# Wq's first half issued ahead of ScalarE's function table, transposed tile 1 loaded by GpSimd's queue

## The reference

```
xn = (x - mean(x)) / sqrt(var(x) + 1e-5)
# branch 1: retrieval from a memory; only every 4th of the 32 heads of q is used
q    = (xn @ Wq.T + bq)[heads 0, 4, 8, ... 28]      # 8 heads of 128
s    = elu(q) + 1
a    = (s @ M) / (s @ z + 1e-6)                     # per head
attn = repeat(a, 4 heads) @ Wo.T
# branch 2: dense layer with int8 weights
dense = xn @ (w * w_scale) + b
out   = x + attn + dense
```

## Time and profile before

| | |
|---|---|
| median of three runs | 237.84 us (237.77 to 237.99) |
| the profiled execution's own time | 237.95 us |
| its span, first to last instruction | 236.1 us |
| TensorE matmul busy | 232.5 us, 98% |
| VectorE busy | 174.0 us, 74% |
| ScalarE busy | 125.2 us, 53% |
| GpSimd busy | 107.4 us, 45% |

### The profile page before, as it was taken

The page is one execution under the profiler, slowest core; times in us unless marked ns, Lnnn a source line. Parts: engine busy times, 40 slices in busy tenths (PEclk is TensorE's granted clock), DMA queues, the critical chain, the costliest instruction groups (busy, mean ns, idle before and its releaser), DMA issues.

```text
span 236.1 us, 3421 instructions
## 1 busy us (share of the span) xinstructions
PE 232.5 (98%) x1037; PEld 188.4 (80%) x1037; DVE 174.0 (74%) x275; ACT 125.2 (53%) x285; POOL 107.4 (45%) x117
## 2 busy tenths in 40 slices
PE   8999999999999999999999999999999999999995
PEld 3688788888888788888888888888888888888895
DVE  2989999897589987997858859585667879362511
ACT  4845358687298386585547253654637445630300
POOL 1029437856932356558350442524045598480000
PEclk9999999999999999999999999999999999999999
DMA  6999999999590144471727272431134456879521
GB/s 227 389 412 414 356 250 254 224 212 218 133 278 17 41 95 130 96 180 48 175 89 178 72 196 77 91 104 39 52 94 97 136 135 159 191 189 182 193 98 44
DMA packets 24081, 38.76 MB, mean 164 GB/s; under 512 B 5440, under 2 KB 13248, under 8 KB 22912
## 3 DMA queue, kind: packets, MB, share of 16 engines
q1 hardware_dynamic: 18816, 26.10, 33.7%
q0 software_dynamic: 3808, 11.14, 24.5%
q10 hardware_dynamic: 1440, 1.31, 1.9%
HBM read 25.95 MB, written 4.19 MB: 128 GB/s over the span
## 4 chain that ended last, share of the span: by engine, by line
PE 98%; DVE 0%; issue 0%
PE attn_ps L876 14%; PE attn_ps L878 14%; PE attn_ps L877 13%; PE q_ps L876 10%; PE q_ps L878 10%; PE q_ps L877 10%; PE dense_ps L876 6%; PE dense_ps L878 6%; PE dense_ps L877 6%; PE dense_ps L967 2%; PE q_ps L916 1%; PE q_ps L904 1%; PE q_ps L911 1%; PE attn_ps L916 1%; PE attn_ps L904 1%; PE attn_ps L911 1%
## 5 line engine op out<-in xcount | busy, mean ns | idle before, releaser
L489 ACT ACTIVATE s<-s,rden 128x128 f32<-128x128 f32 x128 | 39.2, 390 | 39.3 <-DVE rden L707 37.6
L341 POOL TENSOR_TENSOR e_and_sz<-s,z_b 128x512 f32<-128x512 f32 x32 | 41.7, 1340 | 39.6 <-DVE den L703 39.6
L876 PE MATMUL attn_ps<-P_hi,aT_hi 128*128 128x512 f32 (+1 forms) x136 | 53.0, 389 | 0.0
L878 PE MATMUL attn_ps<-P_hi,aT_lo 128*128 128x512 f32 (+1 forms) x136 | 52.2, 384 | 0.0
L877 PE MATMUL attn_ps<-P_lo,aT_hi 128*128 128x512 f32 (+1 forms) x136 | 52.1, 383 | 0.0
L876 PE MATMUL q_ps<-WqT_hi,xT_hi 128*128 128x512 f32 x104 | 40.7, 391 | 0.0
L878 PE MATMUL q_ps<-WqT_hi,xT_lo 128*128 128x512 f32 x104 | 40.5, 389 | 0.0
L877 PE MATMUL q_ps<-WqT_lo,xT_hi 128*128 128x512 f32 x104 | 40.5, 389 | 0.0
L691 DVE SCALAR_TENSOR_TENSOR q_ps<-q_ps,rstd,bq_b 128x512 f32<-128x512 f32 x28 | 21.0, 752 | 17.6 <-PE q_ps L878 17.6
L876 PEld LDWEIGHTS attn_ps<-P_hi,aT_hi 128*128 128x128 f32 x136 | 25.6, 188 | 6.1 <-issue 0.6
L878 PEld LDWEIGHTS attn_ps<-P_hi,aT_lo 128*128 128x128 f32 x136 | 25.6, 188 | 5.2
(11 more groups left out here) (96 smaller groups left out, 356.1 us busy)
## 6 DMA issues: line engine op xcount, KB each, us to landing
x<-in_WoT POOLq DMA_DIRECT2D x6, 1024.0 KB, 11.0
x<-in_b POOLq DMA_DIRECT2D x16, 256.0 KB, 4.4
out<-x SPq DMA_DIRECT2D x15, 256.0 KB, 2.4
x<-in_x SPq DMA_DIRECT2D x14, 256.0 KB, 3.6
xT<-in_xT SPq DMA_DIRECT2D x13, 256.0 KB, 3.8
aT<-s SPq DMA_DIRECT2D x104, 32.0 KB, 2.3
MT<-s SPq DMA_DIRECT2D x72, 32.0 KB, 1.9
x<-in_WoT SPq DMA_DIRECT2D x2, 1024.0 KB, 13.3
```

The source lines that it names most:

```text
L341: nc.gpsimd.tensor_tensor(sz_eps[:, :, h * D // 2:(h + 1) * D // 2].rearrange("p g (j c) -> p j g c", j=2), by_quarter(sbuf_s[:, t % SRING ...
L489: last = nc.scalar.activation(a_g, a_g, ACT.Copy, scale=rden[:, t % 2, g:g + 1])
L876: nc.tensor.matmul(out, x_hi, w_hi, start=start, stop=False)
L878: return nc.tensor.matmul(out, x_lo, w_hi, start=False, stop=stop)
```

## The change

ScalarE issues the load of Wq's half (0, 0) as its very first instruction, ahead of the wait for `warm` and of the function table. Transposed tile 1 leaves ScalarE's queue and becomes the first instruction of GpSimd's list, ahead of the constants. In its place ScalarE issues Wq's half (1, 0), which SP issued third before. SP's queue has one transfer fewer, and all that stands behind it moves up by one place. No arithmetic is changed.

```diff
@@ SyncE
             load_xT(0)
             load_wq_half(0, 1)
-            load_wq_half(1, 0)
             load_wq_half(1, 1)
@@ GpSimd
+            nc.gpsimd.dma_start(xT[:, 1, :, :].rearrange("p k r -> p (k r)"), xT_d[1]).then_inc(xT_in[1], 16)
             nc.gpsimd.memset(mean_weights, 1.0 / HID).then_inc(mean_weights_set, 1)
@@ ScalarE
+            act.dma_start(WqT_raw[:, 0, halves(0)], WqT_d[0, 0][:, halves(0)]).then_inc(wq_half_in[0], 16)
             act.wait_ge(warm_set, 1)
             nc.scalar.activation(table_loaded[:], warm[:, 0:1], ACT.Copy)
-            act.dma_start(WqT_raw[:, 0, halves(0)], WqT_d[0, 0][:, halves(0)]).then_inc(wq_half_in[0], 16)
-            act.dma_start(xT[:, 1, :, :].rearrange("p k r -> p (k r)"), xT_d[1]).then_inc(xT_in[1], 16)
+            act.dma_start(WqT_raw[:, 1, halves(0)], WqT_d[0, 1][:, halves(0)]).then_inc(wq_half_in[2], 16)
             copy_wq_hi(0, 0)
```

## The result

The changed kernel takes 239.27 us (median of six, 239.11 to 239.48), beside 237.98 us before in the same comparison. The ratio is 1.0054, 95% interval 1.0044 to 1.0065: slower by 1.3 us, where I had forecast no change at 237.9 us and a range up to 238.7. The profiled execution took 239.31 us, its span 237.5 us (236.1 before).

The account below looks back on a forecast made before the run. The prediction took TensorE's matmul stream as the bound, its early holes being VectorE's work. Its terms, 0 + 0 + 0 + 0 = 0, left 237.95 us, or 237.84 against the median: forecast 237.9 us, range 237.6 to 238.7.

Parts of the forecast that it names:

- Can this transfer hurt tile 0: Start of the kernel: half (0, 0) issued together with tile 0 delays it by 0, range up to 0.7 to 1.3 us.
- the row of ScalarE's latency: Earlier trace: ScalarE's issue at 169.85 has first packets from 171.05, 1.2 us or more later; from 0.74, 1.94 or later.
- Rival A: VectorE's first addition: half (0, 0) gets in front of tile 0, price 0.7 to 1.3 us, 238.5 to 239.1; chance 0.20.
- The prediction's next paragraph: DMA engines at the start: queues with work take turns by packet; the worst case is the first rival's time.
- TensorE's stream decides: Whole kernel: only TensorE's stream start or holes move the end; about 0.77 us of holes before 10.04 are VectorE's work.
- Half (0, 0) sooner gains 0: ScalarE's start: landing 0.24 us sooner gains 0, since ScalarE would still wait for VectorE at 5.61.
- Tile 1 from GpSimd, value 0: GpSimd's first transfer: issued at 0.74, packets about 2.35; tile 1 has 0.65 us of cover, so value 0.
- Rival B: Tile 1 gets before half (0, 0), or GpSimd's first issue is far slower than 1.6 us: 0.2 to 0.6 us; chance 0.12.
- GpSimd's constants, the table load, half (1, 0): Start: constants have 2.5 us of cover, the table load is hidden before 4.75, half (1, 0) gains nothing; each 0.
- VectorE is full behind it: After the first addition: once tile 0 is more than about 0.05 us late, everything moves with it.

Follow-up runs that it names:

- the half first: Kernels issuing Wq's half (0, 0) ahead of ScalarE's wait and table load, with or without other edits; that edit alone against the kernel before: 239.26 us, again 238.37.
- this part alone: Kernel before with only Wq's half (0, 0) issued ahead of ScalarE's wait and table load: median 239.26 us, ratio 1.0037.
- the kernel with GpSimd held: Changed kernel with GpSimd's product for w waiting until VectorE has made tile 2's low part: median 239.05 us, ratio 1.0038; on another chip 238.91 us.
- the half change: The change without its first part, half (0, 0) issued behind wait and table load as in the kernel before: median 238.47 us, ratio 1.0016.

## Why the prediction was wrong

The step that failed is the one in "Can this transfer hurt tile 0": "I take 0 as the value nearest to the row of ScalarE's latency". The measured value is 1.1 us in the changed kernel's profile, inside the bounds of 0.7 to 1.3 us that the same step gave, and 0.6 to 1.3 us over all profiles with the half first. The experiment with this part alone shows it. Rival A named the place and the price; it had 0.20.

The latency itself was read rightly. The step said that q10's packets come at 1.94 us or later, and in the changed kernel they begin after 2.3 us, in the other profiles with the half first after 2.0. What was wrong is the conclusion, that a queue which comes second costs the first one nothing. By 2.7 us q1 had started only 59 packets (77 with this part alone) where it had started 108, and q10 took its turns while tile 0 was unfinished. I thought of sharing as a matter of who is first; beside q10 tile 0 is slow for as long as both run. The prediction's next paragraph sets out that the queues take turns, which fits these counts; there it stood only as a worst case.

A second term is missing: 239.27 us lies above even rival A's top of 239.1. The prediction put nothing for VectorE's meeting with GpSimd's product, some 0.4 us by the kernel with GpSimd held.

Point by point:

- TensorE's stream decides, and the holes up to 10 us are VectorE's: right. A start 0.82 us later closed the stream 0.81 later, and VectorE was busy for all of that stretch but 0.03 us.
- Half (0, 0) sooner gains 0: right. In the changed kernel's profile it did not even land sooner.
- Tile 1 from GpSimd, value 0: wrong in the half change, by 0.42 us of wait (0.4 us in time). The issue came at 1.27, not 0.74, and the first packet 3.5 us or more after it, not 1.6: the earlier trace rows is a later transfer of that queue. Rival B named just this, a first issue far slower than 1.6 us, and its 0.2 to 0.6 us held. That the value is 0 in the whole change is luck: VectorE, late for another reason, comes to tile 1 at 7.58, after its landing at 7.0.
- GpSimd's constants, the table load, half (1, 0): 0, right as far as the traces show; the matrix for the mean is there at 2.2 us.
- "VectorE is full behind it", so everything moves one for one: incomplete. Two things on the way are not tied to the start. The clock gave back 0.27 us in the profiled execution, and took some more in others. GpSimd's product hangs on a landing; the shifted VectorE fell behind it. The prediction looked for what is hidden beside VectorE's list, not for what may overtake it.
- The sum for rival A: its price of 0.7 to 1.3 us gives a middle of 238.8, not 238.6, so a range up to 238.7 took in a third of A and not its lower half.

The sum as measured in the profiled execution: 1.12 (landing) - 0.30 (clock and the eight zeros' end) + 0.6 (what the lag grows by later, some 0.4 of it the meeting) gives the span's 1.4; the medians differ by 1.29.

## What to carry to other kernels

The first transfer on which all else waits should have the DMA engines to itself: do not issue one of another queue at the same moment. But do not hold the others back far either: here 0.24 us of head start were enough for tile 0, and with 1.5 us the half of Wq landed 4.4 us later and the kernel took 241.41 us. A latency read in the middle of a program held for ScalarE's first transfer and not for GpSimd's. A second queue that comes later than the first still takes its share. When a step on a full engine shifts, look for the instructions of other engines that hang on something that does not shift, above all GpSimd's long ones beside VectorE: a shift of a few tenths of a microsecond that turned the order there went with 1 us. And when two kernels agree in their times, look whether the same thing set both.

## What the runs showed of the hardware

- Two hardware queues with work at the start share the engines: with the half of Wq issued beside tile 0, q1 and q10 started 77 and 36 packets from 1.7 to 2.7 us where q1 alone started 108. Together they could move as much as one: 412 GB/s from 4 to 5 us in the changed kernel. With ScalarE's transfers issued late it was 269 GB/s from 5 to 7 us; why is open.
- A transfer of 256 KB took 2.7, 3.8, 5.7 or 6.8 us to land, by its queue, its moment and what was beside it.
- GpSimd's first transfer of a program: issued 0.5 us after SyncE's although first in its list, first packet 3.5 us later.
- TensorE's rise from 1.2 to 2.4 GHz was over before 5.5 us in one execution of the changed kernel, and in another the first products with Wq, from 7.2 us on, still lay 0.43 us and more apart up to 9.6 us. It was 239.50 against 239.31 us: VectorE's delay by GpSimd hid most of it. The granted clock reads 1.00 in all these stretches, so the pace has to be read from the starts. In the two kernels where TensorE stood idle from 5.8 to 10.12 us and from 5.9 to 8.87 us it fell to 0.50 (1.2 GHz) during the idle time and stayed there until about 15 and 14 us.
